# Gathering only the slots that exist in a last chunk, in the two untyped layers of a graph network kernel

## The chip, the cores and the metric

One core of a Trainium2 chip runs the whole program. The metric is the device time of one execution in microseconds; the kernel before takes 4556.1 us, the median of three runs (4553.02 to 4556.61).

## The reference, cut to what matters

There are 6250 nodes with 256 features and 100000 edges (`src`, `dst`, one of 64 types), drawn at random. Three attention layers run one after the other: two of an untyped network (8 heads, with a feed-forward part), then one typed network (4 heads, no feed-forward part). For each untyped layer:

```
q, k, v = xn @ wq + bq, xn @ wk + bk, xn @ wv + bv          # N x 8 x 32 each
scores = einsum('ehd,ehd->eh', q[dst], k[src]) * scale       # edges, and one self loop per node
ex = exp(scores - segment_max(scores, dst)[dst])
agg = segment_sum((ex / z[dst]) * v[src], dst)
h = h + agg @ wo + bo
h = h + gelu(layernorm(h) @ w1 + b1) @ w2 + b2
```

So for every edge one row of keys and values (512 numbers of 4 bytes, 2 KB) of its source node has to be fetched by index.

## The kernel before, in words

The nodes are sorted by their number of edges and cut into 49 blocks of 128 nodes, one node per partition. A block's edges are laid out as slots: slot s holds the s-th edge of each of the 128 nodes. Four slots make a chunk (`CH`), six chunks a round (`CPS`, 24 slots, `W`). A block has as many chunks as its fullest node needs, and more than one round when that node has over 24 edges. One gather (L1260) is one indirect DMA issued by GpSimd: for one slot, 128 rows of 2 KB from `kv_dram` into the tile `kv`, which holds two rounds (slots of round k lie at `k % 2`). A node with fewer edges gathers row 0 in its empty slots, and the maxima mask these slots.

The number of edges of a block's fullest node follows from the drawn `dst`. In the order in which the blocks run it is 8, 9, 10, 11, 11, 11, 12, 12, 12, 32, 25, 23, 22, 22, 21, 21, 20 (three blocks), 19 (three), 18 (four), 17 (five), 16 (five), 15 (five), 14 (four), 13 (four). In chunks: nine blocks of two or three, one of eight and one of seven (two rounds each), five of six, fifteen of five, eighteen of four. That is 218 chunks or 872 slots a layer. Filled up to whole chunks there are 73 slots a layer that no node of their block has: 7 in the first nine blocks, 3 in the block with 25, 11 in the blocks of six chunks, 27 in those of five, 25 in those of four.

Each engine runs its own loop over the blocks (`iterate`), and the engines meet by semaphores:

- GpSimd (L1274 to L1293), for block b: gather the nodes' own records (`gather_nodes`, L1240), which waits until VectorE is through with the record of block b-4; scatter the new keys and values of block b-5 (`scatter`, L1224), which waits for ScalarE's `record(b - 5)`; then `gather_round` (L1253 to L1270). Before each chunk c it waits for `used` (TensorE has summed the same place two rounds ago) and `taken` (VectorE has passed the wait for the same chunk of the round before).
- VectorE (L1534 to L1609), for block b: `scores`, for each chunk the wait for its four slots (`landed`, L1301), the products of keys and query (L1324), written over the keys in `kv`, and the sums over each head (L1329), where the products of chunk c are issued before the head sums of chunk c-1; then `maxima`; then `second(b - 2)`, which waits for TensorE's feed-forward output `f2` (L1497 in the first layer, L1499 in the second); statistics, the sum of the weights, `even_out`; then `weigh` (L1429), which multiplies the values of each chunk by their weights. After that the next block starts (L1443).
- TensorE for block b: `feed_forward(b - 2)` (L1950), `turn_sums(b - 1)` (L477), `feed_out(b - 2)` (L1963), projections, and last `sums` (L1875), one 128x128 by 128x256 product per slot of a chunk, empty ones included.
- ScalarE: the exponentials, the Gelu between L1950 and L1963 (L1715), normalization, `record` (L1752).

`Blocks.next` (L394) reads a word per block from `block_row` on each engine, which gives the number of earlier rounds and the chunks of the last one. `block_sizes` (L777) makes these words in the prelude. If and else are real branches of an engine's own instruction stream.

## Time and profile before

| | us |
|---|---|
| median of 3 runs | 4556.1 |
| span of the profiled execution | 6464.2 |
| its prelude, up to the first block of layer one | 664 |
| its first layer | 2035 |
| its second layer | 2094 |
| its typed layer | 1671 |

The profiled execution has no time of its own on the page beside its span. It is 1908 us longer than the median of the runs. Busy in that span: TensorE 3974.3 us, VectorE 3512.3, GpSimd 2945.1, ScalarE 1921.7. A row of a timeline gives the start, the duration, engine, line, operation, output and inputs, and how long the engine sat idle before it and for whom.

### The profile page before, as it was taken

The page shows a single profiled execution, that of the slowest core. Times are in us where ns is not written, and L with a number is a line of the kernel's source. Part 1 is how long each engine was busy: PE and PEld are TensorE (multiplying, and loading weights), DVE is VectorE, ACT ScalarE, POOL GpSimd, SP SyncE. Part 2 cuts the span into 40 slices and gives each one's busy share as a digit, 9 for nine tenths or more (in the row PEclk, how much of TensorE's full clock was granted, in tenths as well). Part 3 has the DMA queues.
Part 4 walks back from the last instruction along what each step waited for, and adds up shares of the span by engine and source line. Part 5 has one row for each costly group of instructions (what it writes and reads, how often), then busy time and mean ns, then how long its engine had stood idle before and what let it go on. Part 6 is the DMA issues. An engine that isn't in the chain of part 4 may idle for free. (4 is left out here: it accounts for less than half of the span.)

```text
span 6464.2 us, 95809 instructions
## 1 busy us (share of the span) xinstructions
PE 3974.3 (61%) x17667; PEld 2909.4 (45%) x17668; DVE 3512.3 (54%) x5215; ACT 1921.7 (30%) x4404; POOL 2945.1 (46%) x2969
## 2 busy tenths in 40 slices
PE   8555455666666666565566666666666456666556
PEld 6222343454554444444444444444444345444444
DVE  6431445554554455345555555444446577777666
ACT  3332222222222232332222222222234233333333
POOL 0230445544544444334555444444424466666554
PEclk9777777777777777777777777777787677877777
DMA  3343545555554445444555555444434456665554
GB/s 123 129 116 80 156 133 159 155 156 155 159 161 137 137 143 147 126 128 141 165 161 163 155 147 145 140 140 140 140 107 134 137 163 174 179 173 158 158 148 121
DMA packets 384173, 935.62 MB, mean 145 GB/s; under 512 B 143750, under 2 KB 156256, under 8 KB 384106
## 3 DMA queue, kind: packets, MB, share of 16 engines
q0 software_dynamic: 232080, 751.31, 40.6%
q1 hardware_dynamic: 151708, 182.79, 8.6%
q10 hardware_dynamic: 320, 0.84, 0.0%
q8 instruction: 18, 0.29, 0.0%
q14 instruction: 47, 0.38, 0.0%
HBM read 791.63 MB, written 143.30 MB: 145 GB/s over the span
## 5 line engine op out<-in xcount | busy, mean ns | idle before, releaser
L1260 POOL DMA_INDIRECT kv<-kv_dram,idx x2616 | 2592.1, 991 | 1475.8 <-issue 765.0
L1875 PE MATMUL ps_acc<-kv,ident 128*128 x5232 | 1268.4, 403 | 66.7 <-issue 59.2
L1875 PEld LDWEIGHTS ps_acc<-kv,ident 128*128 128x128 f32 x5232 | 1057.0, 204 | 272.9 <-issue 116.6
L1329 DVE TENSOR_REDUCE sc<-kv 128x32 f32 (+2 forms) x654 | 791.8, 1214 | 366.6 <-issue 351.7
L1950 PE MATMUL ps_big<-xnaT,w_ffn 128*128 128x128 f32 x3136 | 529.5, 302 | 649.2 <-issue 645.4
L1324 DVE TENSOR_TENSOR kv<-kv,ps_q 128x1024 f32 x654 | 786.3, 1215 | 230.3 <-issue 227.3
L1963 PE MATMUL ps_w<-w_ffn,shared 128*128 128x256 f32 x1568 | 558.9, 532 | 396.0 <-ACT shared L1715 336.5
L1429 DVE TENSOR_TENSOR kv<-kv,ps_q x654 | 754.8, 1216 | 49.7 <-issue 40.2
L1950 PEld LDWEIGHTS ps_big<-xnaT,w_ffn 128*128 128x128 f32 x3136 | 450.6, 210 | 699.3 <-issue 687.7
L1963 PEld LDWEIGHTS ps_w<-w_ffn,shared 128*128 128x128 f32 x1568 | 426.0, 279 | 541.3 <-ACT shared L1715 388.1
L1643 ACT COPY agg<-ps_acc 128x256 f32<-128x256 f32 x147 | 54.7, 372 | 1994.6 <-remote 1080.8
L1224 POOL DMA_INDIRECT kv_dram<-rec_out,scatter_to x98 | 100.3, 1024 | 832.2 <-issue 832.2
L1715 ACT ACTIVATE shared<-ps_big,b 128x128 f32<-128x128 f32 x784 | 213.8, 381 | 524.1 <-remote 519.5
L477 PE MATMUL ps_t<-ident,xna 128*128 128x128 f32 x392 | 96.2, 332 | 393.9 <-ACT xna L1720 190.3
L489 PE MATMUL ps_kv<-w_qkv,xnbT 128*128 128x512 f32 x588 | 333.2, 695 | 0.0
L1316 DVE TENSOR_TENSOR kv<-kv,w_ffn x218 | 265.9, 1220 | 43.5 <-issue 30.7
L1240 POOL DMA_INDIRECT rec_in<-in_x,node_at x49 | 49.9, 1019 | 472.0 <-issue 472.0
L1497 DVE TENSOR_TENSOR rec_out<-h,ps_w 128x256 f32 (+1 forms) x49 | 20.6, 421 | 448.8 <-PE ps_w L1963 395.4
L477 PEld LDWEIGHTS ps_t<-ident,xna 128*128 128x128 f32 x392 | 47.1, 157 | 457.1 <-ACT xna L1720 234.5
L1499 DVE TENSOR_TENSOR h<-h,ps_w 128x256 f32<-128x256 f32 x49 | 20.6, 421 | 417.9 <-PE ps_w L1963 388.2
L456 ACT ACT_TABLE_LOAD x96 | 123.2, 1283 | 362.8 <-DVE mv L1520 362.7
L477 PE MATMUL ps_t<-ident,agg 128*128 128x128 f32 x294 | 84.7, 361 | 220.3 <-issue 176.4
(235 smaller groups left out, 5188.7 us busy)
## 6 DMA issues: line engine op xcount, KB each, us to landing
rec_dram<-rec_out SPq DMA_DIRECT2D x98, 512.0 KB
rec_in<-rec_dram SPq DMA_DIRECT2D x98, 512.0 KB
kv<-kv_dram,idx POOLq DMA_INDIRECT x2616
rec_by_node<-rec_in SPq DMA_DIRECT2D x49, 512.0 KB
windows<-kv SPq DMA_DIRECT2D x49, 384.0 KB
kv_dram<-rec_in SPq DMA_DIRECT2D x49, 256.0 KB
rec_out<-in_x SPq DMA_DIRECT2D x48, 128.0 KB
w_ffn<-in_L_gnn_w SPq DMA_DIRECT2D x4, 1024.0 KB
```

The lines of the kernel that those rows point to most:

```text
L456: nc.scalar.activation(sd[:], mv[:, :, 1], ACT.Sqrt, bias=eps_col[:]).then_inc(done, 1)
L477: mm = nc.tensor.transpose(to[:, c, :], of[:, c * P:(c + 1) * P], ident[:])
L489: mm = nc.tensor.matmul(to, ofT[:, c, :], wt[:, c, a:z], start=False, stop=(c == KD - 1))
L1260: pool.indirect_dma_start(kv[:, u * W + slot, :], None, kv_dram[l], bass.IndirectOffsetOnAxis(ap=idx[:, u, slot:slot + 1], axis=0)).then_i ...
L1316: nc.vector.tensor_tensor(at, at, rel_of(k, c).unsqueeze(2).broadcast_to([P, CH, H, DH]), ALU.add).then_inc(s["relk"], 1)
L1324: nc.vector.tensor_tensor(at, at, q, ALU.mult).then_inc(s["mul"], 1)
L1329: nc.vector.tensor_reduce(scw[:, slice(c * CH * H, (c + 1) * CH * H) if isinstance(c, int) else bass.ds(c * (CH * H), CH * H)].rearrange(" ...
L1429: nc.vector.tensor_tensor(at, at, wt.unsqueeze(3).broadcast_to([P, CH, H, DH]), ALU.mult).then_inc(s["weighted"], 1)
L1715: nc.scalar.activation(gT[:, f, :], ps_big[:, f // 4, (f % 4) * P:(f % 4 + 1) * P], ACT.Gelu, bias=b_1[:, l, f:f + 1]).then_inc(s["g"], 1)
L1875: mm = nc.tensor.matmul(ps_acc[:, 0:D], ident[:], at[:, :, slot, :].rearrange("p a d -> p (a d)"), start=False, stop=False, skip_group_che ...
L1950: mm = nc.tensor.matmul(to, w_1[:, c, f * P:(f + 1) * P], xnaT[:, c, :], start=(c == 0), stop=(c == KD - 1))
L1963: mm = nc.tensor.matmul(to, gT[:, f, :], w_2[:, f, :], start=False, stop=(f == KF - 1))
```

## The change

Three things change in the two untyped layers; the typed layer keeps its gathers and its products in place.

1. The word of a block also carries the slots of its last round (`slots`), so that GpSimd and VectorE know how many slots the last chunk has.
2. GpSimd gathers four, three, two or one slots in a last chunk, by nested branches, in chunks after a round's first; chunk 0 is always gathered whole. VectorE's wait for such a chunk asks for 16 increments per gathered slot instead of 64, with the number computed in registers.
3. A slot that isn't gathered keeps older keys and values. The products are therefore no longer written over the keys but into a tile of their own with two halves (`products_of`), used in turn. From the third chunk on the products wait until the head sums of the chunk before last have been read out of the same half (`score`). The tile shares its room with `w_qkv[0]`, which only the prelude reads.

```diff
+WORD = 256
-        w_qkv = [sb(f"w_qkv{l}", [P, KD, 3 * D]) for l in range(3)]
+        products_tile = sb("products", [P, 2 * CH * D])
+        products_of = [products_tile[:, n * CH * D:(n + 1) * CH * D].rearrange("p (s d) -> p s d", d=D) for n in range(2)]
+        w_qkv = [products_tile[:, 0:KD * 3 * D].rearrange("p (c n) -> p c n", c=KD),
+                 *(sb(f"w_qkv{l}", [P, KD, 3 * D]) for l in (1, 2))]
...
+                self.word = both
                 last = nc.s_assert_within(self.eng.snap(both % PACKED), 1, CPS, skip_runtime_bounds_check_because=packed)
-                earlier = nc.s_assert_within(self.eng.snap(both // PACKED), 0, KMAX,
+                earlier = nc.s_assert_within(self.eng.snap(both // WORD), 0, KMAX,
...
+            def slots(self):
+                return nc.s_assert_within(self.eng.snap((self.word // PACKED) % (WORD // PACKED)), 0, W,
+                                          skip_runtime_bounds_check_because="a round has no more slots")
...
-                    def gather_round(u, k, chunks_left):
-                        def gather(c):
+                    def gather_round(u, k, slots_left):
+                        def gather(c, slots):
+                            for slot in range(c * CH, c * CH + slots):
+                                pool.indirect_dma_start(
+                                    kv[:, u * W + slot, :], None, kv_dram[l],
+                                    bass.IndirectOffsetOnAxis(ap=idx[:, u, slot:slot + 1], axis=0)).then_inc(
+                                        kv_sem[c], 16)
+
+                        def free(c):
                             pool.wait_ge(s["used"], k * CPS + c + 1)
                             settle(pool)
                             pool.wait_ge(s["taken"], k * CPS + c + 1)
                             settle(pool)
...
+                        def some(c):
+                            with pool.If(slots_left > c * CH + 1):
+                                with pool.If(slots_left > c * CH + 2):
+                                    gather(c, 3)
+                                    pool.nop()
+                                with pool.Else():
+                                    gather(c, 2)
+                                    pool.nop()
+                                pool.nop()
+                            with pool.Else():
+                                gather(c, 1)
+                                pool.nop()
+
+                        free(0)
+                        gather(0, CH)
+                        for c in range(1, CPS):
+                            with pool.If(slots_left > c * CH):
+                                free(c)
+                                if typed:
+                                    gather(c, CH)
+                                else:
+                                    with pool.If(slots_left >= (c + 1) * CH):
+                                        gather(c, CH)
+                                        pool.nop()
+                                    with pool.Else():
+                                        some(c)
+                                        pool.nop()
+                                pool.nop()
                             pool.nop()
...
-                    def landed(c):
+                    def landed(c, slots=None):
+                        if slots is not None:
+                            dve.reg_alu(rows_left, dve.snap((slots - c * CH) * 16), LANDED, ALU.min)
+                            dve.reg_alu(rows_landed, rows_left, 16, ALU.max)
+                            landings[c].by = dve.snap(rows_landed, min_val=16, max_val=LANDED)
                         landings[c].wait()
+                        landings[c].by = LANDED
                         dve.sem_inc(s["taken"], 1)
...
                         def products(c):
                             if typed:
                                 dve.wait_ge(s["relk"], chunk0 + c + 1)
-                            at = chunk_of(k, c, 0)
-                            nc.vector.tensor_tensor(at, at, q, ALU.mult).then_inc(s["mul"], 1)
+                            at = product(c) if typed else chunk_of(k, c, 0)
+                            if not typed and c >= 2:
+                                dve.wait_ge(s["score"], chunk0 + c - 1)
+                            nc.vector.tensor_tensor(product(c), at, q, ALU.mult).then_inc(s["mul"], 1)
...
-                                chunk_of(k, c, 0).rearrange("p s (h d) -> p s h d", h=H), AX_X,
+                                product(c).rearrange("p s (h d) -> p s h d", h=H), AX_X,
                                 ALU.add).then_inc(s["score"], 1)
...
                             if c:
-                                landed(c)
+                                landed(c, None if typed else slots)
...
                             k, chunk0, filled = last_round(counts)
+                            slots = blocks.slots()
                             start(b)
...
-                            scores(b, k, chunk0, filled, beside)
+                            scores(b, k, chunk0, filled, beside, slots)
```

## Rows read from the trace of the kernel before

**Rows 1.** The page: span, and busy time of each engine.
```profile
span 6464.2 us, 95809 instructions
PE 3974.3 (61%) x17667; PEld 2909.4 (45%) x17668; DVE 3512.3 (54%) x5215; ACT 1921.7 (30%) x4404; POOL 2945.1 (46%) x2969
```

**Rows 2.** Windows of the prelude and the three layers: us, busy us (instructions), PEclk, DMA share.
```profile
0.00:664.00 664.00, 413.35 (x1735) 237.50 (x1736) 266.31 (x662) 208.62 (x543) 110.87 (x117) 0.78 0.37 116
664.00:2699.00 2035.00, 1281.36 (x5327) 948.36 (x5327) 1038.05 (x1512) 560.64 (x1281) 926.32 (x970) 0.78 0.50 146
2699.00:4793.00 2094.00, 1286.44 (x5376) 955.85 (x5376) 1054.32 (x1561) 577.74 (x1341) 929.15 (x973) 0.77 0.50 145
4793.00:6464.00 1671.00, 993.13 (x5229) 767.72 (x5229) 1153.58 (x1481) 574.68 (x1240) 978.72 (x909) 0.74 0.54 155
```

**Rows 3.** Timeline of a four-chunk block, TensorE's feed-forward: fast, then one by one.
```profile
2311.09 2.81 PE L1950 MATMUL ps_big<-xnaT,w_ffn 128*128 128x128 f32 x23
...
2315.59 0.27 PE L1950 MATMUL ps_big<-xnaT,w_ffn 128*128 128x128 f32 x1 [1.15 <-issue]
```

**Rows 4.** Source view of VectorE's chunk branches: count, duration ns min/median/max.
```profile
L1353 DVEq COMPARE_BRANCH  x1206: 2/47/1408, 665.9 to 6424.5; - x173
```

**Rows 5.** Timeline of the same block, GpSimd.
```profile
2306.95 0.96 POOL L1260 DMA_INDIRECT kv<-kv_dram,idx  x1 [0.39 <-issue]
...
2309.47 0.94 POOL L1260 DMA_INDIRECT kv<-kv_dram,idx  x1 [0.30 <-issue]
2310.71 0.95 POOL L1260 DMA_INDIRECT kv<-kv_dram,idx  x1 [0.30 <-issue]
...
2331.00 1.01 POOL L1240 DMA_INDIRECT rec_in<-rec_by_node,node_at  x1 [1.79 <-issue]
...
2345.49 1.03 POOL L1224 DMA_INDIRECT kv_dram<-rec_out,scatter_to  x1 [13.47 <-issue]
```

**Rows 6.** Source view of the prelude's small scatters, a few bytes per row.
```profile
L632 POOL DMA_INDIRECT node_table<-kv x49: 954/958/1117, 237.8 to 298.6; - x49
```

**Rows 7.** Timeline of the same block, VectorE, from one weighing to the next.
```profile
2302.38 4.62 DVE L1429 TENSOR_TENSOR kv<-kv,ps_q  x4 [0.19 <-issue]
...
2308.13 2.35 DVE L1324 TENSOR_TENSOR kv<-kv,ps_q 128x1024 f32 x2 [0.34 <-issue]
2310.39 1.21 DVE L1329 TENSOR_REDUCE sc<-kv 128x32 f32 x1
2311.53 1.21 DVE L1324 TENSOR_TENSOR kv<-kv,ps_q 128x1024 f32 x1
...
2324.59 0.36 DVE L1379 TENSOR_TENSOR sm<-sc,meta 128x192 f32<-128x192 f32 x1 [1.95 <-issue]
...
2325.53 0.37 DVE L1384 TENSOR_TENSOR sm<-sm,mrun 128x200 f32<-128x200 f32 x1
...
2337.35 0.42 DVE L1497 TENSOR_TENSOR rec_out<-h,ps_w 128x256 f32 x1 [11.45 <-PE ps_w L1963]
2337.92 0.43 DVE L1514 BATCH_NORM_STATS2 bns<-rec_out 128x6 f32 x1 [0.15 <-DVE rec_out L1497]
...
2342.18 4.62 DVE L1429 TENSOR_TENSOR kv<-kv,ps_q  x4 [0.19 <-issue]
```

**Rows 8.** Timeline of the same block, the rest of TensorE's way.
```profile
2304.09 7.14 PE L1875 MATMUL ps_acc<-kv,ident 128*128 x32
...
2325.78 0.69 PE L477 MATMUL ps_t<-ident,agg 128*128 128x128 f32 x2 [0.99 <-ACT agg L1643]
...
2330.74 6.39 PE L1963 MATMUL ps_w<-w_ffn,shared 128*128 128x256 f32 x16 [3.95 <-ACT shared L1715]
```

**Rows 9.** Timeline of layer two, VectorE: an operation behind two waits and address registers.
```profile
4038.96 0.43 DVE L1504 TENSOR_TENSOR rec_out<-h,rec_in 128x256 f32 x1 [0.67 <-DVE h L1499]
```

**Rows 10.** DMA view: a queue that carries instructions (packets, MB, share), and a small transfer with us to landing.
```profile
q14 instruction: 47, 0.38, 0.0%
...
slot_index<-idx SPq DMA_DIRECT2D x2, 12.0 KB, 1.4
```

More of the change, by code:

```diff
@@ L396, in next @@
                 sl = slice(2 * b, 2 * b + 1) if isinstance(b, int) else bass.ds(2 * b, 1)
-                both = self.eng.value_load(block_row[0:1, sl], min_val=1, max_val=KMAX * PACKED + CPS)
-                packed = "a word holds a block's rounds but one, times eight, and the chunks of its last round"
+                both = self.eng.value_load(block_row[0:1, sl], min_val=1, max_val=KMAX * WORD + PACKED * W + CPS)
+                packed = "a word holds a block's rounds but one, and the slots and the chunks of its last round"
+                self.word = both
                 last = nc.s_assert_within(self.eng.snap(both % PACKED), 1, CPS, skip_runtime_bounds_check_because=packed)
-                earlier = nc.s_assert_within(self.eng.snap(both // PACKED), 0, KMAX,
+                earlier = nc.s_assert_within(self.eng.snap(both // WORD), 0, KMAX,
                                              skip_runtime_bounds_check_because=packed)
@@ L1312, in scores, with product @@
                             settle(dve)
+                        def product(c):
+                            if typed:
+                                return chunk_of(k, c, 0)
+                            if isinstance(c, int):
+                                return products_of[c % 2]
+                            return products_tile[:, bass.ds((c % 2) * (CH * D), CH * D)].rearrange(
+                                "p (s d) -> p s d", d=D)
                         def add_relation(c):
@@ L1316, in add_relation @@
                             nc.vector.tensor_tensor(
-                                at, at, rel_of(k, c).unsqueeze(2).broadcast_to([P, CH, H, DH]),
+                                product(c).rearrange("p s (h d) -> p s h d", h=H), at, rel_of(k, c).unsqueeze(2).broadcast_to([P, CH, H, DH]),
                                 ALU.add).then_inc(s["relk"], 1)
@@ L1541, in iteration @@
                             k, chunk0, filled = last_round(counts)
+                            slots = blocks.slots()
                             start(b)
```

26 lines of the change are left out of this document (10 added, 16 removed).

## The prediction, made before the changed kernel ran

> **What bounds the kernel now.** I read the page first, then the windows by layer, then the timeline of one four-chunk block engine by engine. The page shows no engine above 61% [rows 1], but that span is 6464 us where the runs take 4556, so the shares say little by themselves. The timeline tells where the 1908 us come from: TensorE issues 23 feed-forward products in 2.81 us (0.12 us each) and then waits 1.15 us "for nothing the profile shows" before a single one [rows 3], and VectorE's chunk branches, 47 ns in the median, reach 1408 ns [rows 4]. In such stretches the instruction streams of all engines crawl while GpSimd's gathers keep their step. I take them for a cost of the profiled execution, spread over 147 blocks: 1908 / 147 = 13.0 us a block. The block of the rows lasts 2342.18 - 2302.38 = 39.8 us from weighing to weighing [rows 7], so 26.8 us in a run. The prelude and the typed layer, 664 and 1671 us of the span [rows 2], are not touched.
>
> Three chains can set a block's length.
>
> GpSimd, with n gathers: one gather follows another after 1.25 us (0.95 and a gap of 0.30), then the record gather 1.01 + 0.3 and the scatter 1.03 + 0.3 [rows 5]. So 1.25n + 2.7: 22.7 us for 16 slots, 27.7 for 20, 32.7 for 24. Bytes don't matter for this: scatters of a few bytes per row take the same 958 ns [rows 6].
>
> The chain across the engines, with c chunks: weighing to first sum 1.7 us [rows 7, 8], sums 7.14 / 4 = 1.8c, 32 feed-forward products at 0.122 = 3.9 [rows 3], transposes 0.69 + 0.2, output products 6.39 + 0.2 [rows 8], and from VectorE's L1497 to the next weighing 4.8 [rows 7]. For four chunks 1.7 + 7.1 + 3.9 + 0.9 + 6.6 + 4.8 = 25.0. The 26.8 above are an upper bound of the same thing; I take 26.0, thus 27.8 for five chunks, 29.6 for six and 24.2 for three.
>
> VectorE's own work: 4.8, weighing 1.15c, 1.1 to the first product, 2 x 1.14 = 2.28c for products and head sums, 1.3 for the maxima [rows 7] and an estimated 0.9 for the branches and waits around them (some ten at the 47 ns of rows 4 and a gap or two). That is 21.8 us for four chunks, 25.2 for five, 28.7 for six.
>
> So blocks of three and four chunks are bound by the chain across the engines with 3 us or more in which GpSimd is idle (its 13.47 us before the scatter in rows 5 are 13 of the profile's and little else). Blocks of five chunks stand at a tie (27.7 against 27.8). The five blocks of six chunks are bound by GpSimd (32.7 against 29.6). They follow the two-round blocks, where the gathers of a round have to wait for the sums two rounds back, so GpSimd enters them with no lead to live on.
>
> **The change part by part.** *Gathers that go*: 73 slots a layer, 146 in all, so L1260 falls from 2616 to 2470 gathers; 146 x 1.25 = 182 us of GpSimd's time, of which only that in bound blocks counts. The 25 slots in four-chunk blocks and 7 in the first nine blocks are worth nothing: 26.0 and 24.2 stay due next. The 27 in five-chunk blocks: GpSimd falls to 27.7 - 1.25 to 27.7 - 3.75, the chain at 27.8 stays; 0 here, 0.9 us in each of the twelve blocks that lose a slot, or 11 us a layer, if the chain is really 25.0 at four chunks and so 26.8 at five. The six-chunk blocks lose 1, 2, 2, 3, 3 slots: GpSimd 31.5, 30.2, 30.2, 29.0, 29.0; the chain 29.6 is next, VectorE's own work with its new waits (below) 29.9. The gain is 1.2 + 2.5 + 2.5 + 2.8 + 2.8 = 11.8 us a layer. The three slots of the block with 25: its second round waits for the sums, but the gathers behind it start earlier; 0 to 3.7 us, I take 1.
>
> *The wait of the products* for `score`: from the third chunk on, a product can only start when the head sums just issued have ended. VectorE now starts the next operation 1.14 us after one of 1.21 us [rows 7], 0.07 before its end. Behind a wait it starts 0.15 us after the end at the nearest row [rows 7], and 0.67 us after it where two waits and address registers stand between [rows 9]. So 0.2 to 0.7 us a chunk; I take 0.3, since here one wait and one address stand between. Behind it are queued the products, then the head sums of the chunk before, and nobody else waits. It makes 0.6 us in a four-chunk block, 0.9 in five, 1.2 in six: 22.4, 26.1 and 29.9 us. Only the six-chunk blocks feel that, counted above, and the first rounds of the two-round blocks, 1.2 each: 2.4 us a layer lost.
>
> *VectorE's registers* for each landing: some three more instructions at 50 to 150 ns (the chunk branch has 47 [rows 4]), issued while 2.28 us of work are queued: hidden; if they aren't, 0.3 us a chunk. The tile of products instead of `kv`: the operations have the same shape, 0, and -0.1 to +0.1 us each as bounds. `slots` is read while the weighing runs (4.62 us [rows 7]): hidden.
>
> *GpSimd's branches*: one or up to three more per chunk. Its stream runs ahead of the gather in progress, so a gather of 0.95 us covers them; uncovered 0.2 us a chunk. Fewer bytes (6% of the gathers) ease the DMA engines, whose share is 0.50 [rows 2]; nothing waits for that.
>
> Sum: -(11.8 + 1 - 2.4) = -10.4 us a layer, -21 in two layers, 4535; rounded by the small terms that may not be hidden to **4536 us** (-0.4%). This sum is made on the runs' own time by the subtraction of 13 us a block, since the span can't be compared; in the profiled execution GpSimd waits anyway, and I expect its span to move less than 1%.
>
> *Instruction pages.* The trace shows 47 packets of instructions with 0.38 MB, 8 KB each [rows 10], in 6464 us and so none for most blocks: the block loops stay loaded. GpSimd's loop in an untyped layer has about 206 instructions before, a gather being two; after the change every chunk but a round's first has 30 instead of 12, in two copies, about 390 in all. The Trainium skill, "Runtime: NRT & Kernel Launch", section "Instruction fetch mechanics", says that most engines hold 512 instructions in a few pages and that a taken branch to a page that isn't held stalls until it is fetched. By that page 390 instructions fit only if the pages fall well, and it speaks against the change; no run here shows a loop of that length. The rival below prices it.
>
> **The rivals.**
> - *Nothing that counts* (near 4552). The change takes its gathers away, but GpSimd isn't late: if a gather in a run costs 1.10 us or less instead of 1.25, six chunks take 29.1 and are level with the chain. For it: the gap of 0.30 us may belong to the profile, as the crawling does. Against: it is as steady inside crawling stretches as outside [rows 5]. That the change doesn't remove the gathers at all I hold for all but excluded.
> - *VectorE becomes the bound* (slower). Place: `scores` in five- and six-chunk blocks. Price: at 0.3 us a wait 0.9 x 15 + 1.2 x 7 = 22 us a layer, +44, with nothing gained from the gathers: about 4598. At the upper bound of 0.7 it is 4655. It decides if VectorE's own work is already above 27.8 at five chunks, 2.6 us more than I add up. For it: my 0.9 for branches is soft. Against: VectorE waited 11.45 us for TensorE at L1497 in the rows [rows 7], about 3 us more than TensorE's crawl alone would leave.
> - *GpSimd's loop no longer stays loaded* (slower). Place: the jump back to the loop's start and into the second copy. Price: three pages a block, each as a small transfer of 12 KB that took 1.4 us to land [rows 10], 4.2 us on GpSimd: five chunks 27.7 - 2.2 + 4.2 = 29.7 against 27.8, 1.9 x 15 = 28 us a layer; six chunks 32.7 - 2.7 + 4.2 = 34.2, 1.5 x 5 = 8; in sum +72, 4628. Below 2 us a block it vanishes in the tie. This is the result that the Trainium skill's "Instruction fetch mechanics" would give.
>
> **How the numbers follow.** Chances: forecast 0.46, nothing that counts 0.26, VectorE 0.15, instruction pages 0.13. The forecast's own range is 4492 to 4547: at its low end the chain is 1 us shorter (11 us more a layer in five-chunk blocks, up to 0.6 a block more in the six), the block with 25 gives 3.7, the waits cost nothing: 32 us a layer. At its high end the waits cost 0.7 and take back all but 9 us. The range of 8 in 10 is 4490 to 4600; it takes in the VectorE case at its middle and leaves out its upper end and most of the pages. The measurement can tell about 0.2%, 9 us, from no change. Faster 0.46; same 0.27; slower 0.27, the two slower rivals less the part in which they cost under 9 us, plus a little of the middle one.
>
> **What would show it.** 2470 gathers at L1260 with 1.25 us from one to the next. Head sum to product 0.2 to 0.4 us apart from the third chunk on, instead of overlapping. In six-chunk blocks VectorE's wait for landings gone. The instruction queue still near 50 packets; hundreds would mean the pages. If L1324 or L1329 have other durations than 1.21 us, the tile matters after all. The prediction falls if blocks of four chunks change their length, which none of my terms touches, or if the gain comes near 100 us: then GpSimd binds five-chunk blocks too.

## The result, and the profile after

The changed kernel takes 4503.4 us in the median of four runs (4497.1 to 4511.6); the kernel before, beside it on the same chip, 4556.4 us (4553.0 to 4557.1). The ratio is 0.9889 (95%: 0.9875 to 0.9903): 53 us less, where 21 was forecast. Faster was right; the size was not, and 4503 lies inside the range of 4490 to 4600.

The 6464 us of [rows 1] were a disturbed execution: the kernel before, profiled once more, has a span 2 us short of its time. That second trace is the "before" of every comparison from here on. Its page, answering [rows 1, 10] (engines: busy us, share, instructions; the instruction queue as packets, MB and share; then the feed-forward's output product, busy us and mean ns):

```profile
span 4555.2 us, 95809 instructions
PE 3580.3 (79%) x17667; PEld 2690.9 (59%) x17668; DVE 3492.5 (77%) x5215; ACT 1928.6 (42%) x4404; POOL 2959.5 (65%) x2969
...
q14 instruction: 46, 0.38, 0.0%
...
L1963 PE MATMUL ps_w<-w_ffn,shared 128*128 128x256 f32 x1568 | 364.6, 386 | 0.1
```

and the source view of VectorE's branches, answering [rows 4] (ns: minimum, median, maximum), where 1408 has become 69:

```profile
L1353 DVEq COMPARE_BRANCH  x1206: 43/47/69, 567.3 to 4514.9; - x173
```

The same of the changed kernel, whose lines are 8 to 56 further down: L1260 is now L1268, L1324 L1377, L1329 L1382, L1429 L1482, L1950 L2006, L1963 L2019.

```profile
span 4501.1 us, 96621 instructions
PE 3554.8 (79%) x17667; PEld 2674.4 (59%) x17668; DVE 3506.9 (78%) x5216; ACT 1928.3 (43%) x4404; POOL 2831.6 (63%) x2829
...
q14 instruction: 288, 2.36, 0.2%
...
L1268 POOL DMA_INDIRECT kv<-kv_dram,idx x2476 | 2464.9, 996 | 851.6 <-issue 726.7
...
L2019 PE MATMUL ps_w<-w_ffn,shared 128*128 128x256 f32 x1568 | 364.7, 386 | 0.1
```

Three things stand out. The gathers fell by 140, not 146: the three missing slots of the block with 25 lie in chunk 0 of its last round, and chunk 0 is always gathered whole. The product at L1963 takes 386 ns in the mean in both, where the first trace had 532 ns and 6.39 us for sixteen of them [rows 8]; its line was:

```profile
L1963 PE MATMUL ps_w<-w_ffn,shared 128*128 128x256 f32 x1568 | 558.9, 532 | 396.0 <-ACT shared L1715 336.5
```

And the instruction queue carries 288 packets instead of 46.

By layers (columns as in [rows 2]), before and then after:

```profile
566.00:1887.00 1321.00, 1121.31 (x5327) 860.03 (x5327) 1028.96 (x1512) 566.21 (x1281) 926.28 (x970) 0.92 0.75 225
1887.00:3217.00 1330.00, 1129.24 (x5380) 866.46 (x5381) 1045.67 (x1560) 585.18 (x1345) 927.70 (x970) 0.92 0.75 227
3217.00:4555.00 1338.00, 923.94 (x5228) 729.43 (x5225) 1151.48 (x1482) 568.90 (x1235) 986.52 (x913) 0.80 0.65 194
```

```profile
570.00:1865.00 1295.00, 1111.35 (x5327) 854.45 (x5327) 1036.31 (x1511) 566.18 (x1281) 860.30 (x900) 0.92 0.72 216
1865.00:3159.00 1294.00, 1115.17 (x5377) 856.74 (x5377) 1052.31 (x1561) 585.09 (x1345) 863.48 (x900) 0.93 0.71 219
3159.00:4501.00 1342.00, 920.65 (x5228) 727.71 (x5228) 1151.87 (x1482) 568.72 (x1236) 988.82 (x913) 0.80 0.65 194
```

The gain lies in the two untyped layers, 26 and 36 us; the prelude and the typed layer are 4 us longer each. Both untyped layers lose the same 70 gathers; why the first gains 10 us less is the second question of this study.

The counts of gathers in the trace also correct two numbers given before: of the 73 slots that no node has, 8 lie in the first nine blocks and 26 in the blocks of five chunks, not 7 and 27. The total and the sum of the forecast don't change by it.

Where the 36 us of layer two come from, by blocks (mean distance in us from one L1443 to the next, of all blocks whose fullest node has so many slots; in the changed kernel that line is L1496):

| slots of the block | blocks | before | after | saved in all |
|---|---|---|---|---|
| 13 (four chunks; the last block has no next) | 3 of 4 | 23.17 | 22.77 | 1.2 |
| 14 to 16 | 14 | 22.56 to 22.90 | 22.29 to 22.65 | 4.4 |
| 17 | 5 | 27.97 | 25.93 | 10.2 |
| 18 | 4 | 27.70 | 25.93 | 7.1 |
| 19 | 3 | 27.68 | 26.46 | 3.7 |
| 20 | 3 | 27.10 | 27.04 | 0.2 |
| 21, 22 | 4 | 32.77, 33.04 | 29.85, 30.42 | 11.1 |
| 23 | 1 | 34.15 | 32.60 | 1.6 |

Five-chunk blocks give 21.2 us, where the forecast had 0; six-chunk blocks 12.7, where it had 11.8. (The rest of the layer is 3 us longer.)

VectorE in a block of five chunks of layer two, before:

```profile
2624.58 5.75 DVE L1429 TENSOR_TENSOR kv<-kv,ps_q  x5 [0.15 <-issue]
...
2638.18 1.21 DVE L1329 TENSOR_REDUCE sc<-kv 128x32 f32 x1
2641.89 1.22 DVE L1324 TENSOR_TENSOR kv<-kv,ps_q 128x1024 f32 x1 [2.50 <-DMA kv<-kv_dram,idx]
...
2652.26 1.22 DVE L1429 TENSOR_TENSOR kv<-kv,ps_q  x1 [0.18 <-issue]
```

and GpSimd in the same stretch:

```profile
2635.47 0.94 POOL L1260 DMA_INDIRECT kv<-kv_dram,idx  x1 [0.30 <-PE ps_acc L1875]
2636.72 0.94 POOL L1260 DMA_INDIRECT kv<-kv_dram,idx  x1 [0.30 <-issue]
2637.97 1.02 POOL L1240 DMA_INDIRECT rec_in<-in_x,node_at  x1 [0.30 <-issue]
2639.29 1.03 POOL L1224 DMA_INDIRECT kv_dram<-rec_out,scatter_to  x1 [0.30 <-issue]
```

VectorE waits 2.50 us for the last chunk to land, while GpSimd goes from gather to gather with its constant 0.30 us, record gather and scatter too: nothing holds it up, it is the bound. This goes for the blocks of four chunks too: in layer one, from the first block of five chunks to the start of the last block (998.7 to 1799.2 us), and in layer two alike, none of GpSimd's 636 gathers and scatters has more than 0.31 us before it. The 17 distances between blocks of four chunks are 22.7 us in the mean in layer one and 22.8 in layer two, and 1.25 x 16 + 2.7 = 22.7. The block of the rows lasts 27.68 us, and 1.25 x 20 + 2.7 = 27.7. A block of five chunks of the changed kernel:

```profile
2575.71 5.75 DVE L1482 TENSOR_TENSOR kv<-kv,ps_q  x5 [0.17 <-issue]
...
2584.87 1.21 DVE L1382 TENSOR_REDUCE sc<-products 128x32 f32<-128x1024 f32 x1
2586.25 1.22 DVE L1377 TENSOR_TENSOR products<-kv,ps_q 128x1024 f32<-128x1024 f32 x1 [0.16 <-DVE sc L1382]
2587.39 1.21 DVE L1382 TENSOR_REDUCE sc<-products 128x32 f32<-128x1024 f32 x1
...
2601.64 1.22 DVE L1482 TENSOR_TENSOR kv<-kv,ps_q  x1 [0.19 <-issue]
```

The wait for the landing is gone, the block lasts 25.93 us, and VectorE is never idle for another engine: it is now the bound, with the new wait before each product from the third chunk on (from 2586.08, the end of the head sums, to 2586.25). The forecast had written 26.1 for exactly this sum.

### The profile page after: what moved, and what is told of

Read it like the earlier page. It is cut to its first block and busy times, and to the rows that moved or that the text cites. A ratio compares the mean times of both kernels' runs of the same rounds, so it can differ in the third digit from the quotient of the medians.

```text
span 4501.1 us, 96621 instructions
## 1 busy us (share of the span) xinstructions
PE 3554.8 (79%) x17667; PEld 2674.4 (59%) x17668; DVE 3506.9 (78%) x5216; ACT 1928.3 (43%) x4404; POOL 2831.6 (63%) x2829
## 3 DMA queue, kind: packets, MB, share of 16 engines
q14 instruction: 288, 2.36, 0.2%
## 5 line engine op out<-in xcount | busy, mean ns | idle before, releaser
L1268 POOL DMA_INDIRECT kv<-kv_dram,idx x2476 | 2464.9, 996 | 851.6 <-issue 726.7
L1482 DVE TENSOR_TENSOR kv<-kv,ps_q x654 | 753.5, 1215 | 26.9 <-issue 17.4
L1377 DVE TENSOR_TENSOR products<-kv,ps_q 128x1024 f32<-128x1024 f32 x436 | 524.3, 1220 | 149.8 <-DMA kv<-kv_dram,idx 82.5
L1382 DVE TENSOR_REDUCE sc<-products 128x32 f32<-128x1024 f32 (+1 forms) x436 | 521.3, 1212 | 5.0 <-issue 4.1
L2006 PE MATMUL ps_big<-xnaT,w_ffn 128*128 128x128 f32 x3136 | 374.2, 278 | 2.8 <-ACT xnaT L1764 2.8
L2006 PEld LDWEIGHTS ps_big<-xnaT,w_ffn 128*128 128x128 f32 x3136 | 358.0, 192 | 14.8 <-issue 3.5
L2019 PE MATMUL ps_w<-w_ffn,shared 128*128 128x256 f32 x1568 | 364.7, 386 | 0.1
L2019 PEld LDWEIGHTS ps_w<-w_ffn,shared 128*128 128x128 f32 x1568 | 290.1, 190 | 47.1 <-ACT shared L1771 0.4
L1377 DVE TENSOR_TENSOR kv<-kv,ps_q 128x1024 f32 x218 | 264.5, 1213 | 48.5 <-DMA kv<-kv_dram,idx 46.7
L1382 DVE TENSOR_REDUCE sc<-kv 128x16 f32 (+1 forms) x218 | 264.4, 1213 | 12.6 <-DVE kv L1377 12.6
L1925 PE MATMUL ps_acc<-acc_scaled,ident 128*128 128x256 f32 x306 | 133.9, 532 | 144.0 <-DVE acc_scaled L1446 144.0
L498 PE MATMUL ps_kv<-w_qkv,xnbT 128*128 128x512 f32 x392 | 195.3, 621 | 0.0
```

The lines of the kernel that those rows point to most:

```text
L498: mm = nc.tensor.matmul(to, ofT[:, c, :], wt[:, c, a:z], start=False, stop=(c == KD - 1))
L1268: pool.indirect_dma_start(kv[:, u * W + slot, :], None, kv_dram[l], bass.IndirectOffsetOnAxis(ap=idx[:, u, slot:slot + 1], axis=0)).then_i ...
L1377: nc.vector.tensor_tensor(product(c), at, q, ALU.mult).then_inc(s["mul"], 1)
L1382: nc.vector.tensor_reduce(scw[:, slice(c * CH * H, (c + 1) * CH * H) if isinstance(c, int) else bass.ds(c * (CH * H), CH * H)].rearrange(" ...
L1482: nc.vector.tensor_tensor(at, at, wt.unsqueeze(3).broadcast_to([P, CH, H, DH]), ALU.mult).then_inc(s["weighted"], 1)
L1925: nc.tensor.matmul(ps_acc[:, 0:D], ident[:], acc_scaled[:], start=True, stop=False, skip_group_check=True)
```

## The experiments

All times are medians beside the kernel before on the same chip. A ratio is estimated from the single runs and can differ by 0.1% from the quotient of the two medians.

**The kernel before once more.** No edit.

> The kernel before once more, for a second trace; the time is 4553 to 4557 us. The first trace's span was 6464 us, that of the changed kernel 4501. If the crawling stretches belonged to that one execution, this span comes near 4555, and the blocks can be compared without subtracting anything. Theory A (GpSimd binds four-chunk blocks too): four-chunk blocks with 16 gathers last 22.7 us or a little more, five-chunk blocks 27.7, six 32.7. Theory B (the prediction's: the chain across the engines binds four-chunk blocks at 25 to 26 us): 25 to 26, 27.8, 32.7.

Time 4557.1 us, span 4555.2; its rows are above. So the extra time of the first trace isn't what recording a profile costs. Every number that the prediction took from a stretched row is open again. Of the two theories A holds: blocks with 16 gathers last 22.7 and 22.8 us in the mean, those with 20 gathers 27.1 to 28.0, those with 24 32.8 to 34.2.

**Which part brings what.** First all chunks gathered whole, so that the words of the blocks, the tile and its wait are all that is left of the change:

```
-                                if typed:
+                                if True:
                                     gather(c, CH)
...
-                                landed(c, None if typed else slots)
+                                landed(c)
```

> The changed kernel with every last chunk gathered whole again (2616 gathers) and the full wait, so only the tile of products, its wait and the longer words are left of the change. Theory A: GpSimd binds, so the wait is hidden behind it: 4550 to 4565 us. Theory B, with 0.3 us a wait hidden but in six-chunk and two-round blocks: 4556 to 4562. Rival C (VectorE's own work is near the bound and the wait eats a part of the gain): 4570 to 4600.

4555.4 against 4552.0 us, ratio 1.0004 (0.9995 to 1.0013). Without fewer gathers there is no gain, and tile and wait cost nothing that can be seen while GpSimd sets the length of the blocks.

Then the other way round, the fewer gathers with the products in place, as before. Slots that aren't gathered then hold keys multiplied by older queries; the maxima mask them.

```
-                            if typed:
-                                return chunk_of(k, c, 0)
-                            if isinstance(c, int):
-                                return products_of[c % 2]
-                            return products_tile[:, bass.ds(...)]...
+                            return chunk_of(k, c, 0)
...
-                            if not typed and c >= 2:
-                                dve.wait_ge(s["score"], chunk0 + c - 1)
```

> The changed kernel with the products written over the keys again and without their wait, so only the shorter gathers are left. Part of the computation changes: a slot that isn't gathered holds keys multiplied by queries of earlier blocks; it is masked afterwards. Theory A or B, wait hidden: the changed kernel's time, 4498 to 4505 us. Rival C (the wait costs 0.3 us from the third chunk on and VectorE's own work sets the blocks once the gathers are shorter): 30 to 50 us less, 4455 to 4475.

4482.0 us, ratio 0.9849 (0.9834 to 0.9864), against 0.9889 with the tile (0.987 in a second measurement, further down): once the gathers are fewer, the wait costs 10 to 20 us. That lies between the two ranges that were expected, below the 30 to 50 us of rival C. VectorE in a five-chunk block of this kernel:

```profile
2594.34 1.21 DVE L1375 TENSOR_REDUCE sc<-kv 128x32 f32 x1
2595.47 1.21 DVE L1370 TENSOR_TENSOR kv<-kv,ps_q 128x1024 f32 x1
2596.60 1.21 DVE L1375 TENSOR_REDUCE sc<-kv 128x32 f32 x1
```

The product starts 0.08 us before the head sums end, where the changed kernel starts it 0.17 us behind the end: 0.25 us a wait. Three of them stand in a five-chunk block, and blocks with 17 and 18 slots last 25.32 us here instead of 25.93.

**Which blocks bring it.** Only chunks up to the fourth gathered short, or only the fifth and sixth. The first edit is shown, the second has `c >= 4` in its place:

```
-                                if typed:
+                                if typed or not (c <= 3):
                                     gather(c, CH)
...
-                                landed(c, None if typed else slots)
+                                landed(c, slots if not typed and (c <= 3) else None)
```

> The changed kernel with short gathers only in a round's second to fourth chunk, so that only blocks of up to four chunks gather less (33 of the 70 slots a layer). GpSimd's loop has 313 instructions. Four-chunk blocks last 22.3 to 22.9 us before as after, so these slots are worth next to nothing: 4545 to 4557 us if the loop stays loaded (a rival: four-chunk blocks are bound by GpSimd's 22.7 and gain up to 0.5 us each, 4535). If 313 instructions are already fetched anew each block in layer one, 20 us or so more.

> The changed kernel with short gathers only in a round's fifth and sixth chunk, so that only blocks of five and six chunks gather less (37 of the 70 slots a layer). The loop has 277 instructions. The second traces of the kernel before and of the changed one differ in layer two by 33 us in these blocks (27.7 to 25.9 or 26.5 for five chunks, 33.0 to 30.0 for six), so 2 x 33 = 66 us: 4485 to 4495, faster than the full change, because the loop stays loaded. A rival: the gain hangs on the lead that GpSimd builds up in the other blocks, then 4510 or more.

Up to the fourth: 4556.8 against 4551.0, ratio 1.0011 (1.0002 to 1.0021), nothing gained in sum. In its trace the blocks of layer one with 13 to 15 slots do last 21.7 us instead of 22.6 to 23.4, and layer one is 10 us shorter; against that the typed layer, where nothing is changed, is 17 us longer (1355 instead of 1338), some 1.0 us in each of its four-chunk blocks (24.2 to 24.3 us instead of 23.3), and why is not known. So this run doesn't price the slots of four-chunk blocks by its time. From the fifth on: 4472.4, ratio 0.983 (0.9815 to 0.9845): the whole gain of the changed kernel and more, and 13 us faster than the fastest that was expected, 4485. What was left out on GpSimd can't have brought that, and the page shows what did: 47 packets in the instruction queue in both, not 288. GpSimd's loop over the blocks has 386 instructions in the changed kernel, 313 and 277 in these two, 206 before.

**The instruction pages.** GpSimd with one branch a slot instead of four nested copies, everything else as changed; its loop has 235 instructions:

```
-                                    with pool.If(slots_left >= (c + 1) * CH):
-                                        gather(c, CH)
-                                        pool.nop()
-                                    with pool.Else():
-                                        some(c)
-                                        pool.nop()
+                                    gather(c, 1)
+                                    for n in range(1, CH):
+                                        with pool.If(slots_left > c * CH + n):
+                                            gather(c, n + 1, n)
+                                            pool.nop()
```

> The changed kernel with GpSimd's nested branches replaced by one branch a slot: the same gathers, but a loop of about 235 instructions instead of 385. The changed kernel's trace has 288 packets in the instruction queue where before had 47, 252 of them in layer one's loop and 11 in layer two's, at 1295 and 1294 us for these layers. Theory D (fetched pages cost GpSimd time): packets back to about 50 and layer one faster by 20 us or more. Theory E (the fetches are hidden, since layer one is no slower than layer two): packets back to about 50, time within 5 us of the changed kernel's 4503.

4466.1 us, ratio 0.9805 (0.9792 to 0.9819); layer one 1267 us instead of 1295, layer two 1299 instead of 1294 (on that the last section). Its instruction queue is back to 46 packets:

```profile
q14 instruction: 46, 0.38, 0.0%
```

That could also be the merit of the branches themselves. So the loop was left as it is and only shifted in memory. The first attempt put 64 register moves ahead of the loops of the layers:

```
                 settle(pool)
+                unused = pool.alloc_register("unused")
+                for n in range(64):
+                    pool.reg_mov(unused, n)
```

> The changed kernel with 64 register moves ahead of GpSimd's layer one, which do nothing but shift its three loops by half of an 8 KB page; they cost some 4 us once, beside other work. If the fetches in layer one's loop and their absence in layer two's come from where the 385 instructions lie in the pages, the counts change: layer one falls from 252 to about 12 with a gain of about 25 us, or layer two rises to about 250 and loses as much. If they come from something else in layer one, 252 and 11 stay, 4503 us.

The compiler dropped moves that nobody reads, so this is the changed kernel a second time: 4492.5 us, ratio 0.987 (0.9855 to 0.9885), 288 packets again. It tells nothing of the shift, but how far two measurements of one program lie apart, 0.2%. In its trace layer two is 10 us longer than in the first one of the changed kernel (1304 and 1294 us). Semaphore increments aren't dropped (32 is shown; 75, 128, 16 and 104 stand in the same place):

```
                 settle(pool)
+                for _ in range(32):
+                    settle(pool)
```

> The changed kernel with 32 semaphore increments ahead of GpSimd's layer one, which nothing waits for. (In f3 the compiler dropped the 64 moves: GpSimd's program there is the changed kernel's, to the byte.) They shift all later loops by a quarter of an 8 KB page of 128 instructions and cost some 3 us once. Theory P (place): layer one's loop of 386 instructions happens to touch five pages, is fetched page by page in each block (252 packets / 49 blocks = 5.1), and layer two's touches four, which fit. A loop of 386 touches five pages of 128 only when it starts on a page's last instruction or so, hence 32 more free it: layer one near 12 packets, layer two still 11, 4475 to 4485 us. Theory Q (something else in layer one): 252 and 11 as before, 4492 to 4506 us.

> As g1, with 75 increments. Layer two's loop starts 437 instructions behind layer one's, 53 behind it in a page of 128, so under theory P these 75 put layer two's loop where layer one's was: layer one near 12 packets, layer two near 250, 4500 us. Theory Q: 252 and 11 as before.

With 32 ahead: 4473.7 us, ratio 0.9813 (0.9797 to 0.983), with the loop of 386 instructions untouched. Layer one (first row) is as short as with the short loop, 55 us shorter than before, and 29 shorter than the changed kernel's 1295:

```profile
565.00:1831.00 1266.00, 1102.70 (x5327) 845.93 (x5327) 1035.91 (x1512) 566.19 (x1281) 861.77 (x900) 0.94 0.73 220
1831.00:3123.00 1292.00, 1115.29 (x5377) 855.37 (x5377) 1052.24 (x1561) 585.11 (x1345) 864.10 (x900) 0.93 0.71 219
```

and its instruction queue:

```profile
q14 instruction: 48, 0.39, 0.0%
```

The 288 packets of the changed kernel lie in one place: 252 within layer one, 5.1 a block, 11 in layer two. What a block's fetches do to GpSimd in layer one, in the changed kernel and then with 32 instructions ahead (a block's last gather, the record gather, and the scatter):

```profile
1521.26 0.95 POOL L1268 DMA_INDIRECT kv<-kv_dram,idx  x1 [0.30 <-issue]
1526.10 1.02 POOL L1252 DMA_INDIRECT rec_in<-rec_by_node,node_at  x1 [3.90 <-issue]
...
1550.30 1.01 POOL L1252 DMA_INDIRECT rec_in<-rec_by_node,node_at  x1 [2.90 <-issue]
1551.81 1.03 POOL L1236 DMA_INDIRECT kv_dram<-rec_out,scatter_to  x1 [0.50 <-issue]
```

```profile
1480.26 1.02 POOL L1254 DMA_INDIRECT rec_in<-rec_by_node,node_at  x1 [0.30 <-issue]
1481.59 1.03 POOL L1238 DMA_INDIRECT kv_dram<-rec_out,scatter_to  x1 [0.30 <-DVEq L1348]
```

Where the loop jumps back to its start GpSimd stands still for 2.1 to 3.9 us in these blocks of the changed kernel, 0.30 with the shift. Not every block shows it there: of the 48 later record gathers of layer one, 26 have 0.6 to 10.2 us before them, 78 us in sum, and 22 have 0.30; with the shift one has 4.8, all others 0.30.

The 75 were chosen to put layer two's loop, which starts 437 instructions behind layer one's, where layer one's had been bad. They gave 4477.2 us, ratio 0.982 (0.9804 to 0.9837), and 12 and 11 packets in the layers, so nothing fetched block by block in either: that expectation missed. Whether the place was missed by an instruction or two, or is not the whole of it, stays open.

Next the long loop without fewer gathers. The number of slots is rounded up to whole chunks in the register, so GpSimd runs the nested branches, but always takes the whole chunk:

```
-                            slots_left = pool.snap((earlier - j) * W + slots, ...)
+                            slots_left = pool.snap((earlier - j) * W + ((slots + 3) // CH) * CH, ...)
...
-                                landed(c, None if typed else slots)
+                                landed(c)
```

> The changed kernel with the slots rounded up to whole chunks as the program runs, so that GpSimd has the long loop with its nested branches but makes all 2616 gathers. Beside e2 (the same gathers, a loop of 206 instructions, 4555 us, 46 packets) this is the price of the long loop where GpSimd binds most blocks. If a block's fetches cost GpSimd about 1 us in layer one, 40 to 50 us: 4600; if most of it is hidden behind gathers in progress, 4560 to 4575. Packets near 288.

4592.1 against 4557.5 us, ratio 1.0068 (1.0051 to 1.0084); 288 packets. Against the whole gathers with the short loop (1.0004) the fetches cost 0.64%, 29 us, between the two prices that were expected; layer one is 1357 us long instead of 1322, layer two the same 1334 to 1335. This is the third rival by itself: a change like this one that had brought nothing would have come out slower by its loop alone.

Last the period. A packet has 2.36 MB / 288 = 8.2 KB; if it holds 128 instructions, a shift by 128 puts the loop at the same place of such a piece.

> As g1, with 128 increments ahead, one whole page of 128 instructions (8 KB), so every loop of GpSimd lies as in the changed kernel relative to the pages. 32 and 75 freed layer one (13 and 12 packets, 4474 and 4477 us), but 75 didn't bring the fetches to layer two, so the place in the page is not settled. Theory P (place within a page decides): layer one is back at about 250 packets, 4500 to 4512 us (the increments cost some 5 us once at most). Theory R (any shift, or the increments themselves, frees the loop; for example it only matters what the program ahead of it has left loaded): about 12 packets, 4475 to 4482 us.

> The kernel of h1 once more, for its time: on h1's chip the kernel before took 6361 to 6480 us, so its 6294 can't be set beside the other runs. Layer one near 250 packets as there, 4500 to 4512 us where the kernel before takes 4550 to 4558.

> As g1 with 16 increments. 0 and 128 leave layer one with 252 fetches, 32 and 75 free it. If the loop only just touches a fifth page (a loop of 386 instructions can do so at one or two of 128 places), 16 free it: about 12 packets, 4475 us. If GpSimd needs the page behind the loop's last one as well, a wide range of places is bad, and 16 may still fetch: 250 packets, 4505 us.

> As g1 with 104 increments. By the narrow rule (one or two bad places of 128) about 12 packets in both layers, 4477 us. By the wide one (all but some 60 places are bad for each layer) layer one or layer two has 250.

The first of these ran on a chip on which the kernel before took 6361 to 6480 us, and this one 6294 (ratio 0.9753, 0.9686 to 0.9821); its time says nothing of the shift, but its packets do, 253 in layer one. On another chip: 4511.7 us, ratio 0.9905 (0.9889 to 0.9922), 252 packets in layer one:

```profile
q14 instruction: 289, 2.37, 0.2%
```

One run each with 16 and 104 ahead: 4466.6 and 4474.4 us beside 4552.7, 13 packets in layer one. So for layer one's loop 0 and 128 are bad places, 16, 32, 75 and 104 are good ones. That fits a narrow bad place that comes back after 128 instructions; that it does so every 128, and that the place is all that counts, is not shown, since layer two's loop was not fetched where its count of 437 puts it at a bad place.

**Both costs taken away.** One branch a slot, and the products in place (the two edits above together):

> One branch a slot on GpSimd (4466 us by itself) together with the products written over the keys and without their wait (4482 by itself). As there, a slot that isn't gathered holds keys multiplied by queries of earlier blocks and is masked. If the two costs lie on different engines and add up: 4466 - 21 = 4445 us. If the wait only showed because the fetches made blocks longer, or the two hide each other: 4460 to 4466.

4445.7 against 4551.0 us, ratio 0.9773 (0.976 to 0.9787), the fastest of all. Against one branch a slot alone it is 15 us by the ratios and 19 by the medians, within the 10 to 20 that the products in place gave before: the two costs are separate and add up. It computes what the kernel before computes as long as the masks hide whatever an empty slot has become; a slot that is multiplied by a query once a block and not gathered anew for many blocks holds values without a bound, a risk with other inputs (not tested) that the tile of products avoids.

## Why the prediction was right and wrong

**What bounds the kernel.** Here is the step that failed: "I take them for a cost of the profiled execution, spread over 147 blocks: 1908 / 147 = 13.0 us a block", and then a chain of rows from that execution. The 13 us were a sound correction for the time, but the rows that went into the chain across the engines were not corrected. Its term "output products 6.39 + 0.2" is the mis-sized one, and by it blocks of four chunks were given to the chain, with "3 us or more in which GpSimd is idle", where the undisturbed trace has it idle for no more than 0.31 us at a time in these blocks. Undisturbed, the same sixteen products take 3.72 us; the feed-forward takes 3.82 where the forecast had 3.9, the two transposes 0.38 where it had 0.69 (start, us, line):

```profile
1224.55 3.82 PE L1950 MATMUL ps_big<-xnaT,w_ffn 128*128 128x128 f32 x32
...
1228.73 3.72 PE L1963 MATMUL ps_w<-w_ffn,shared 128*128 128x256 f32 x16
```

Part of it was in the rows: 16 products in 6.39 us are 0.40 us each in a group whose mean was 532 ns, while L1950 was corrected to its fast stretch of 0.122 us a product. The granted clock was 0.78 in the layers of the first trace [rows 2] and is 0.92 now. With 3.72 for 6.39 the chain is 25.0 - 2.7 = 22.3 us at four chunks, 24.1 at five, 25.9 at six. In the trace it is a little shorter still. In the block of four chunks below (layer one, kernel before) VectorE is late by it, since it waits for the output products, and from weighing to weighing it is 21.7 us:

```profile
1475.21 4.62 DVE L1429 TENSOR_TENSOR kv<-kv,ps_q  x4 [0.19 <-issue]
...
1492.07 0.42 DVE L1497 TENSOR_TENSOR rec_out<-h,ps_w 128x256 f32 x1 [0.45 <-PE ps_w L1963]
...
1496.91 1.22 DVE L1429 TENSOR_TENSOR kv<-kv,ps_q  x1 [0.18 <-issue]
```

Where gathers are fewer and nothing is fetched, layer one's blocks of 13 to 15 slots last 21.6 us (32 instructions ahead), with the wait of the products or without it. The prediction had 25.0, and rounded it up to 26.0 by an upper bound from the same span (26.8), which moved it further off.

**GpSimd's term held.** 1.25n + 2.7 gives 22.7 us for 16 gathers, 27.7 for 20 and 32.7 for 24; measured 22.7 and 22.8 in the mean, 27.1 to 28.0 and 32.8 to 34.2. What the prediction called a tie at five chunks (27.7 against 27.8) was a bound by GpSimd, with the corrected chain 3.6 us and VectorE 2.5 us under it.

**VectorE's term held** in layer two, the estimate of 0.9 for branches included: 25.2 us at five chunks, measured 25.32 without the waits; with them 26.1 against 25.93, and at six chunks 29.9 against 29.85 (21 slots). Layer one, whose `second` has one operation in place of L1499 and L1504 with their gap, is some 0.6 us shorter (25.3 us with the waits and 24.7 without, in blocks of 17 slots), which the sum didn't tell apart. VectorE is what is late next in long blocks, as in the second rival's picture, but at 1.6 us below GpSimd, not above it.

**Gathers that go.** "The 25 slots in four-chunk blocks ... are worth nothing" nearly holds in layer two (3.5 us in blocks of 13 to 15 slots), not in layer one: there the blocks of 15, 14 and 13 slots get shorter by 1.3, 1.0 and 1.8 us, some 16 us in all, once nothing is fetched. GpSimd had 22.7 there, the chain 21.6. The prediction had named just this as a sign that it falls, "if blocks of four chunks change their length". In six-chunk blocks 11.8 forecast, 12.7 measured. In five-chunk blocks 0 forecast and 21.2 measured. By the same rule, the larger of GpSimd and VectorE, the corrected sum for layer two is: 17 slots 1.25 x 17 + 2.7 = 24.0, so VectorE's 26.1, saves 27.7 - 26.1 = 1.6, five times; 18 slots (25.2) the same, four times; 19 slots 26.5, saves 1.2, three times: 18 us, and with 11.8 some 30 us a layer; layer two gave 36, layer one 55 without fetches. The prediction's own range had this case at its edge: "the chain is 1 us shorter (11 us more a layer in five-chunk blocks"; it was 3.7 us shorter than the value taken. (The terms named for that edge, 11.8, 11, 3.0 and 3.7, make 29.5 us a layer, not 32, so 4497 and not 4492.) Its last sentence also named the sign by which it would fall, a gain near 100 us, "then GpSimd binds five-chunk blocks too"; they do, and 105 us are gained once fetches and waits are gone.

**The wait of the products.** 0.3 us taken, 0.25 measured, and nothing while GpSimd bounds (e.g. 1.0004 with whole gathers). But with GpSimd out of the way it costs 10 to 20 us, most of it in layer two (1278 us without it, 1294 with it; 0.6 us in each block of 17 or 18 slots), where 4.8 was forecast beside the six-chunk blocks' share. The duration of the operations on the new tile is unchanged, 1.21 and 1.22 us. Words and registers cost nothing that can be seen.

**The rivals.** *Nothing that counts* fell with whole gathers at 1.0004 against 0.9889. *VectorE becomes the bound* is true of its place and false of its sign (and its price of 44 us makes 4600, not 4598). *GpSimd's loop no longer stays loaded* happened, at a chance of 0.13, in one of the two layers: five packets a block where three were thought, 2.1 to 3.9 us of standstill in the blocks shown where 4.2 was priced, none to be seen in nearly half of the others, and in sum 26 to 38 us (the changed kernel's 0.987 and 0.9889 against 0.9813 and 0.9805), where 72 was priced for two layers. It didn't make the kernel slower since GpSimd had just been relieved; with whole gathers it did (1.0068). So the 53 us are some 85 us from fewer gathers, waits included (4473.7 with 32 instructions ahead), less some 30 of fetches in layer one; the forecast of 21 was short of the one and without the other. That 4503 lies inside the ranges is luck to that extent: without the fetches, which the forecast had left to a rival, it would have been some 4474, below both of them.

Of the Trainium skill's "Runtime: NRT & Kernel Launch", section "Instruction fetch mechanics", the runs bear out that a taken branch to code that isn't held waits for its fetch (2.9 and 3.9 us before the record gathers shown), and what the prediction worked out from it, that 386 instructions fit only by their place. They don't bear out its blocks of 16 KiB, which it gives 256 instructions each: the packets have 8.2 KB, and a shift by 128 instructions brought the fetches back. That the 512 instructions it names are four blocks of 128, and that 386 touch a fifth only at a narrow range of places, would give that picture and five packets a block; it is worked out, not shown, and layer two with 75 ahead speaks against its being all.

## What to carry to other kernels

Before a sum is made from a trace, compare its span with the runs: if it is far longer, the rows of every engine are suspect, and a correction of the total alone leaves the terms wrong. Where two chains come out at a tie, the forecast hangs on the smaller error of the two, and both outcomes need a price. A loop whose body is written out in nested copies has a price in instructions, which a timeline of the engine shows only at the loop's head; the packets of the instruction queue, by layer, are where to look, and the same work written with a branch per item was free of them.

## What was not expected of the hardware

- The same program takes 4556 us on most chips and 6361 to 6480 on one, and had a span of 6464 in the first trace. There branches of 47 ns reach 1408 instead of 69, the granted clock in the untyped layers is 0.78 and 0.77 instead of 0.92, and GpSimd's gathers keep their 1.25 us. What sets it is open.
- Whether GpSimd's loop of 386 instructions is fetched anew in each block of layer one, at 0.6 us of a block's time in the end (29 us over 49 blocks), hangs on its place in memory: 0 and 128 instructions ahead of it yes, 16, 32, 75 and 104 no.
- A wait of VectorE on its own last operation costs 0.25 us: 0.17 of a gap, and the 0.08 by which the next operation would have started before the end.
- Layer two with one branch a slot is no shorter than with the nested copies (1299 us against 1292 to 1294), though its loop is. The traces show where the time goes: seven of its blocks of four chunks last 23.7 to 23.8 us instead of 22.3, against two such blocks in the changed kernel's trace, and again seven in the trace of the same program with the dropped moves (layer two 1304 us). In such a block TensorE gets a lower granted clock for a stretch. Here are the sums of a block of 22.3 us, then those of the next, where VectorE comes to wait for TensorE's output product:

```profile
2897.30 0.60 PE L1924 MATMUL ps_acc<-acc_scaled,ident 128*128 128x256 f32 x2
2897.73 7.14 PE L1930 MATMUL ps_acc<-kv,ident 128*128 x32
...
2918.85 0.44 PE L486 MATMUL ps_t<-ident,xna 128*128 128x128 f32 x2 [1.44 <-ACT xna L1775]
...
2919.79 1.06 PE L1924 MATMUL ps_acc<-acc_scaled,ident 128*128 128x256 f32 x2
2920.65 8.15 PE L1930 MATMUL ps_acc<-kv,ident 128*128 x32
```

```profile
2936.60 0.42 DVE L1551 TENSOR_TENSOR h<-h,ps_w 128x256 f32<-128x256 f32 x1 [1.38 <-PE ps_w L2018]
```

The mean granted clock from 2878.20 to 2900.57 us is 1.00, in the next two stretches of a block's length 0.92 and 0.93. TensorE had idled 1.44 us before its transposes when the clock fell, and 1.47 us a block earlier, when it didn't. In layer one's blocks of 21.6 us the clock is 1.00 throughout. Of the two kernels with fewer gathers and the products in place neither has such a block in layer two (22.1 to 22.2 us in all behind the first, which has 24.4); why the clock falls beside the waits and not without them is open.
